# Keys, values and output weights split once and kept as halves in a scratch (one-core attention and expert layer)

## The chip, the cores and the metric

The kernel runs on one core of one Trainium2 chip; the chip's other cores do nothing. The metric is the device time of one execution in microseconds. The kernel before takes 2874.76 us (median of 3 runs, 2874.28 to 2878.58).

## The reference

x is (2, 2048, 2048), in all 4096 tokens of 2048 features, float32 throughout.

```python
xn = _layernorm(x, axis=-1)
# attention, one head, d = 512
qkv = einsum('bsc,cf->bsf', xn, Wqkv) + bqkv
attn = softmax(einsum('bqd,bkd->bqk', q, k) / sqrt(512))
out = einsum('bqd,dc->bqc', einsum('bqk,bkd->bqd', attn, v), Wo) + bo
# experts: 64 of rank 8, the best 16 gated by a softmax over q_r keys
z_gated = (xn @ A_w.T).reshape(..., 64, 8) * gate[..., None]
ffn = einsum('bsn,on->bso', z_gated, B_w) * (32 / 16)
x + out + ffn
```

## The kernel before

Every large product is taken in three passes, so that it comes out in nearly full precision: each float32 operand is split into a high part (rounded to fp32r by a ScalarE copy) and a low part (operand minus high part, a VectorE subtraction), and TensorE adds hi times hi, hi times lo and lo times hi into one PSUM bank (`three`, L1556 to L1558).

Phase A (`phase_a`, about the first 1377 us) normalizes x, multiplies by the joined weights and leaves k, q, v and z (the ungated, then gated expert activations) in DRAM scratches. The change does not touch it, except that its last items already start the first loads of phase B.

Phase B (`phase_b`) works through 8 turns t of 512 queries (`QG`); turns 0 to 3 belong to the first batch of 2048 tokens, turns 4 to 7 to the second. A turn has 32 items, in this order on TensorE:

- scores: 8 key items (K0 to K7 in this text), each 256 keys by 512 features;
- output of the turn before (u = t - 1): 16 items (O0 to O15), four for each block of 512 output columns: two with B_T for the expert part and two with Wo for the attention part. Turn 0 has none; the output of turn 7 comes at the very end;
- values: 8 value items (V0 to V7), each 256 keys by 512 features.

The softmax of turn t lies beside the output items of turn t - 1 (`softmax_step`): running maximum on VectorE, spread over the partitions by TensorE, subtraction of the maximum on VectorE (L1753), exponential on ScalarE (L1459), running sum on GpSimd (L1700). GpSimd also adds the output bias to the loaded x (L1691), and VectorE evicts the output banks with that sum (L1796).

Every item streams one operand through a ring of four slots (`RING`): SyncE loads 512 KB into `r_raw` (`fetch`, L1346), ScalarE makes `r_hi` (L1437), VectorE makes `r_lo` (L1725), TensorE multiplies and counts `b_used`. The fetch of item n waits until `r_lo` of item n - 4 is made; the ScalarE copy of item n waits until TensorE is done with item n - 4. Keys and values of a batch are thus loaded and split again in each of its four turns, and Wo and B_T in each of eight outputs: 256 items. All engines work through orders written out in the code; each engine's queue is served strictly in order. SyncE's queue also holds the loads of x into `res` (L1369), of z (L1406) and of the queries (L1350), and the stores of the result (L1361). `segments` runs turns 0 and 1 written out, turns 2 to 6 in a hardware loop, and turn 7 and the last output written out.

Of the kernel before, what the change touches and what calls it, by code (L numbers as in the profile page):

```python
# [20 lines left out]
F32 = mybir.dt.float32  # L21
# [3 lines left out]
P = 128  # L25
BANKS = 8
W = 512
# [3 lines left out]
def static(v):  # L31
    return isinstance(v, int)
# [28 lines left out]
def layer_kernel(nc, x, xT, W_blocks, b_cols, Wo, bo, B_T, WqT, keysT, out):  # L61
    T, C = x.shape
    D = Wo.shape[0]
    NE, RD = keysT.shape[1], keysT.shape[0]
    RANK = D // NE
    NB = 2
    S = T // NB
    KT = C // P
    TG = 1024
    NG = T // TG  # L70
    QG = 512
    NQ = T // QG
# [8 lines left out]
    stat_scr = nc.dram_tensor("stat_scratch", [NG, 2, TG], F32, kind="Internal").ap()  # L81
    t_scr = nc.dram_tensor("t_scratch", [4, 2, C // 2, W], F32, kind="Internal").ap()

    with ExitStack() as whole:
        def sb(name, shape, dt=F32):
            return whole.enter_context(nc.sbuf_tensor(name, shape, dt))

        psum = whole.enter_context(nc.psum_tensor("psum", [P, BANKS, W], F32))
        common = {
            "ident": sb("ident", [P, P]),  # L90
            "ones": sb("ones", [P, P]),
            "b_col": sb("b_col", [P, 3 * D // P]),
        }
        ahead = Programs()
# [3 lines left out]
        second = phase_b(nc, whole, psum, common, first, ahead, x, Wo, bo, B_T, k_scr, q_scr, z_scr, v_scr, out,  # L98
                         T, C, D, S, QG, NQ, KEYT, DT)
# [12 lines left out]
        @block.tensor  # L112
        def _(pe):
            first.tensor(pe)
            second.tensor(pe)

        @block.gpsimd
        def _(pool):
            first.gpsimd(pool)
            second.gpsimd(pool)  # L120

        @block.vector
        def _(dve):
            first.vector(dve)
            second.vector(dve)
# [1080 lines left out]
    return first  # L1206


def phase_b(nc, whole, psum, common, first, ahead, x, Wo, bo, B_T, k_scr, q_scr, z_scr, v_scr, out,
            T, C, D, S, QG, NQ, KEYT, DT):  # L1210
    RING = 4
    S_IT, O_IT, V_IT = KEYT // 2, 16, KEYT // 2
# [21 lines left out]
    def sem(name):  # L1234
        return whole.enter_context(nc.semaphore(name))
# [23 lines left out]

    b_const = sem("b_const")  # L1260
    b_raw = [sem(f"b_raw{i}") for i in range(RING)]
    b_hi = sem("b_hi")
    b_lo = sem("b_lo")
    b_used = sem("b_used")
# [42 lines left out]
    def uses(t, it):  # L1307

        n = number(t, it)
        if static(n):  # L1310
            return n // RING + 1
        return t * (PER // RING) + (it - O_IT) // RING + 1

    def segments(engine, scores, output, values):


        scores(0)
        values(0, True)
        scores(1)
        output(0, True)  # L1320
        values(1, True)
        with engine.Fori(2, NQ - 1) as t:
            scores(t)
            output(t - 1, True)
            values(t, True)
        scores(NQ - 1)
        output(NQ - 2, True)
        values(NQ - 1, False)
# [7 lines left out]
    def out_ready(engine, u, c, j):  # L1336
        if j < QT - 1:
            engine.wait_ge(b_o, u * CB * (QT - 1) + c * (QT - 1) + j + 1)
        else:
            engine.wait_ge(b_used, number(u + 1, S_IT + c * OPB + OPB - 1) + 1)  # L1340

    def sync(sp, early=False):
        def fetch(t, it, source):
            slot = it % RING
            wait(sp, b_lo, number(t, it) - RING + 1)
            sp.dma_start(r_raw[:, slot, :].rearrange("p (a w) -> p a w", a=source.shape[1]),  # L1346
                         source).then_inc(b_raw[slot], 16)

        def queries(t):
            sp.dma_start(q_raw[:], q_scr.rearrange("(m p) t -> p m t", p=P)[:, :, bass.ds(t * QG, QG)]  # L1350
# [46 lines left out]
        def values(t, more):  # L1397
            base = batch_base(t)
            for i in range(V_IT):
                fetch(t, S_IT + O_IT + i, v_scr[bass.ds(base + i * 2 * P, 2 * P), :]  # L1400
                      .rearrange("(a p) w -> p a w", p=P))
                if i == 0:
                    if static(t) and t == 0:
                        first.stored(sp)
                    wait(sp, b_zt, QT * t)
                    sp.dma_start(z_raw[:], z_scr[bass.ds(t * QG, QG), :]  # L1406
                                 .rearrange("(a p) w -> p a w", p=P)).then_inc(b_z, 16)
                    if more:
                        wait(sp, b_qlo, 2 * (t + 1))
                        queries(t + 1)  # L1410
                if not (static(t) and t == 0):
                    if i == 0:
                        store_block(t - 1, CB - 2)
                    if i == 4:
                        store_block(t - 1, CB - 1)

        if early:
            first.early_stored(sp)
# [135 lines left out]
    def tensor(pe):  # L1554
# [165 lines left out]

    def vector(dve, step=None):
        def split(t, it):
            slot = it % RING
            dve.wait_ge(b_hi, number(t, it) + 1)
# [191 lines left out]
```

## Time and profile before

| | |
|---|---|
| timed runs, median | 2874.76 us |
| profiled execution, its own time | 2878.93 us |
| its span, first to last instruction | 2877.1 us |
| mean granted clock of TensorE | 0.987 |
| TensorE (PE) busy | 2764.0 us, 96% |
| VectorE (DVE) busy | 1776.8 us, 62% |
| ScalarE (ACT) busy | 1053.9 us, 37% |
| GpSimd (POOL) busy | 425.0 us, 15% |
| HBM read, written | 390.74 MB, 83.91 MB |

The span is cut by the profile in 40 equal slices with the busy tenths of each engine; TensorE is at 9 tenths or more in nearly all of them from the sixth on, with a dip around 1440 us, which is turn 0 of phase B. The start-to-start distance of two matmuls in a full stretch is 0.227 us; their ends are modelled, and they overlap, so a single one reads 0.39 us.

### The profile page before, as it was taken

The numbers are of one execution on the slowest core, as the hardware profiler recorded it, in microseconds if no ns is written. First come the engines' busy times: TensorE is split into PE (matmuls) and PEld (weight loads), VectorE is DVE, ScalarE is ACT, GpSimd is POOL, SyncE is SP. The second block draws the span as 40 slices with busy tenths as digits, with TensorE's granted clock in tenths as the row PEclk, the third lists the DMA queues.
The fourth block names the chain that finished last, engine by engine and source line by source line (L and its number), as shares of the span: only waits on it lengthen the run. The fifth ranks groups of instructions, "written<-read, shape, count | busy, mean of one in ns | idle before, by whom it ended". The sixth has DMA issues, their size and how long they took to land.

```text
span 2877.1 us, 34126 instructions
## 1 busy us (share of the span) xinstructions
PE 2764.0 (96%) x12096; PEld 2249.8 (78%) x12096; DVE 1776.8 (62%) x2083; ACT 1053.9 (37%) x1354; POOL 425.0 (15%) x293
## 2 busy tenths in 40 slices
PE   6888999999999999999889999999999999999999
PEld 4676878878888888888778787887878878788787
DVE  6675876467646776455575666546566565565663
ACT  3552325522373223223343343333433334333331
POOL 0011000000000000000022405015041060320611
PEclk9899999999999999999999999999999999999999
DMA  7589765455555463324524534445344453444544
GB/s 296 180 314 301 231 199 191 146 164 174 190 198 142 143 201 121 103 95 154 176 88 139 183 107 163 148 149 186 102 155 151 138 191 116 142 162 128 183 132 139
DMA packets 263276, 476.35 MB, mean 166 GB/s; under 512 B 25328, under 2 KB 74608, under 8 KB 258928
## 3 DMA queue, kind: packets, MB, share of 16 engines
q1 hardware_dynamic: 229104, 387.13, 41.5%
q10 hardware_dynamic: 28288, 66.62, 6.7%
q0 software_dynamic: 5760, 20.97, 2.0%
q8 instruction: 74, 1.21, 0.2%
q14 instruction: 50, 0.41, 0.0%
HBM read 390.74 MB, written 83.91 MB: 165 GB/s over the span
## 4 chain that ended last, share of the span: by engine, by line
PE 81%; DVE 8%; DMA 4%; ACT 3%; issue 3%; POOL 1%; ACTq 0%; SPq 0%; DVEq 0%; POOLq 0%
PE psum L749 36%; PE psum L1556 14%; PE psum L1558 14%; PE psum L1557 14%; DVE prob L1753 2%; PE psum L686 2%; DVE r_lo L1725 2%; ACT r_hi L1437 1%; DMA stat_scratch<-mv 1%; DMA w_raw<-t_scratch 1%; DVE res L1796 1%; DMA rows<-x 1%; DVE w_lo L799 1%; PE psum L1676 0%; ACT w_hi L478 0%
## 5 line engine op out<-in xcount | busy, mean ns | idle before, releaser
L799 DVE TENSOR_TENSOR w_lo<-w_raw,w_hi 128x1024 fp32r<-128x1024 f32 x224 | 274.1, 1224 | 432.3 <-ACT w_hi L478 432.2
L478 ACT ACTIVATE w_hi<-w_raw 128x1024 fp32r<-128x1024 f32 x224 | 237.4, 1060 | 775.8 <-PE psum L749 681.9
L1725 DVE TENSOR_TENSOR r_lo<-r_raw,r_hi 128x1024 fp32r<-128x1024 f32 x256 | 384.1, 1514 | 189.7 <-ACT r_hi L1437 189.7
L1556 PE MATMUL psum<-r_hi,f_hi 128*128 128x512 f32 x1024 | 406.6, 397 | 27.6 <-DVE r_lo L1725 26.2
L1558 PE MATMUL psum<-r_hi,f_lo 128*128 128x512 f32 x1024 | 402.1, 393 | 0.0
L1557 PE MATMUL psum<-r_lo,f_hi 128*128 128x512 f32 x1024 | 402.1, 393 | 0.0
L749 PE MATMUL psum<-s_hi,w_hi 128*128 128x512 f32 x896 | 353.9, 395 | 27.5 <-DVE w_lo L799 15.8
L749 PE MATMUL psum<-w_hi,s_hi 128*128 128x512 f32 x896 | 351.9, 393 | 16.0 <-DVE w_lo L799 14.9
L749 PE MATMUL psum<-s_lo,w_hi 128*128 128x512 f32 x896 | 351.4, 392 | 0.0
L749 PE MATMUL psum<-w_lo,s_hi 128*128 128x512 f32 x896 | 351.2, 392 | 0.0
L749 PE MATMUL psum<-s_hi,w_lo 128*128 128x512 f32 x896 | 351.1, 392 | 0.0
L749 PE MATMUL psum<-w_hi,s_lo 128*128 128x512 f32 x896 | 351.0, 392 | 0.0
L1691 POOL TENSOR_TENSOR res<-res,b_out 128x512 f32<-128x512 f32 x128 | 219.9, 1748 | 664.2 <-DMA res<-x 664.2
L1437 ACT ACTIVATE r_hi<-r_raw 128x1024 fp32r<-128x1024 f32 x256 | 264.0, 1049 | 140.4 <-PE psum L1558 85.0
L1556 PEld LDWEIGHTS psum<-r_hi,f_hi 128*128 128x128 f32 x1024 | 194.1, 190 | 80.8 <-DVE r_lo L1725 24.3
L1558 PEld LDWEIGHTS psum<-r_hi,f_lo 128*128 128x128 f32 x1024 | 194.2, 190 | 41.4
L1557 PEld LDWEIGHTS psum<-r_lo,f_hi 128*128 128x128 f32 x1024 | 194.1, 190 | 39.3
L749 PEld LDWEIGHTS psum<-s_hi,w_hi 128*128 128x128 f32 x896 | 169.7, 189 | 68.9 <-issue 15.9
L1556 PE MATMUL psum<-p_hi,r_hi 128*128 128x512 f32 x512 | 208.1, 406 | 12.7 <-DVE p_lo L1845 8.0
L749 PEld LDWEIGHTS psum<-w_hi,s_hi 128*128 128x128 f32 x896 | 169.6, 189 | 56.6 <-DVE w_lo L799 16.9
L1700 POOL TENSOR_TENSOR run_sum<-prob 128x512 f32<-128x512 f32 x8 | 10.3, 1290 | 1367.8 <-ACT prob L1459 1367.8
L1558 PE MATMUL psum<-p_hi,r_lo 128*128 128x512 f32 x512 | 201.7, 394 | 0.0
(137 smaller groups left out, 4267.3 us busy)
## 6 DMA issues: line engine op xcount, KB each, us to landing
w_raw<-t_scratch SPq DMA_DIRECT2D x128, 512.0 KB, 4.0
w_raw<-W_blocks SPq DMA_DIRECT2D x96, 512.0 KB, 3.8
r_raw<-k_scratch SPq DMA_DIRECT2D x64, 512.0 KB, 3.8
r_raw<-v_scratch SPq DMA_DIRECT2D x64, 512.0 KB, 4.5
r_raw<-B_T SPq DMA_DIRECT2D x64, 512.0 KB, 3.9
res<-x SPq DMA_DIRECT2D x128, 256.0 KB, 4.8
r_raw<-Wo SPq DMA_DIRECT2D x64, 512.0 KB, 4.4
out<-res SPq DMA_DIRECT2D x128, 256.0 KB, 3.4
```

The lines of the kernel that those rows point to most:

```text
L478: nc.scalar.activation(w_hi[:, s % RAW], w_raw[:, s % RAW], ACT.Copy).then_inc(s_whi, 1)
L686: mm = pe.matmul(psum[0:M_R, bank, :], wq[:, block_k + k, :], t[:, k, :], start=(k == 0 and n == 0), stop=(k == HK - 1 and n == 1))
L749: mm = pe.matmul(psum[:, bank, :], stationary, moving, start=(k == 0 and n == 0 and not chained), stop=(k == HK - 1 and n == 2), skip_grou ...
L799: nc.vector.tensor_tensor(w_lo[:, s % RAW], w_raw[:, s % RAW], w_hi[:, s % RAW].bitcast(F32), ALU.subtract).then_inc(s_wlo, 1)
L1437: nc.scalar.activation(r_hi[:, slot, :], r_raw[:, slot, :], ACT.Copy).then_inc(b_hi, 1)
L1556: pe.matmul(bank, sh, mh, start=first, stop=False)
L1557: pe.matmul(bank, sh, ml, start=False, stop=False)
L1558: return pe.matmul(bank, sl, mh, start=False, stop=last)
L1691: nc.gpsimd.tensor_tensor(res[:, slot, :], res[:, slot, :], b_out[:, c * W:(c + 1) * W], ALU.add).then_inc(b_xb, 1)
L1725: nc.vector.tensor_tensor(r_lo[:, slot, :], r_raw[:, slot, :], r_hi[:, slot, :].bitcast(F32), ALU.subtract).then_inc(b_lo, 1)
L1753: nc.vector.tensor_tensor(prob[:, i, :], prob[:, i, :], max_all[:], ALU.subtract).then_inc(b_sub, 1)
L1796: nc.vector.tensor_tensor(res[:, tile % XO, :], psum[:, O_BANK[tile], :], res[:, tile % XO, :], ALU.add).then_inc(b_oev, 1)
```

## The change

A new DRAM scratch, `split_scr`, has a place for the two halves of 48 tiles. An item is split (`is_split`) as before where it is met first: the keys and values in turns 0 and 4, the output weights in turn 1. Behind the split, SyncE stores both halves (`keep`, two transfers of 512 KB). In all other turns SyncE loads the two halves from the scratch straight into `r_hi` and `r_lo`, once TensorE is done with the item four back and the stores out of that slot have landed; no ScalarE or VectorE instruction belongs to such an item, and TensorE waits for the landing itself. Items that are split wait on ScalarE for the stores of their slot too. `segments` has turn 4 written out between two hardware loops (turns 2 and 3, turns 5 and 6).

```diff
+    def is_split(t, it):
+        if not static(t) or t == NQ:
+            return False
+        if OUT_AT <= it < VAL_AT:
+            return t == 1
+        return t % BATCH == 0
...
+        turn(1)
+        LATE["loop"] = False
+        with engine.Fori(2, BATCH) as t:
+            turn(t)
+        turn(BATCH)
+        LATE["loop"] = True
+        with engine.Fori(BATCH + 1, NQ - 1) as t:
+            turn(t)
...
     def sync(sp, early=False):
+        def keep(t, it):
+            slot = it % RING
+            sp.wait_ge(b_lo, split_number(t, it) + 1)
+            for half, r in enumerate((r_hi, r_lo)):
+                sp.dma_start(split_scr[home(t, it), half], r[:, slot, :].bitcast(F32)).then_inc(b_keep[slot], 16)
...
         def fetch(t, it, source):
             slot = it % RING
-            wait(sp, b_lo, number(t, it) - RING + 1)
-            sp.dma_start(r_raw[:, slot, :].rearrange("p (a w) -> p a w", a=source.shape[1]),
-                         source).then_inc(b_raw[slot], 16)
+            if is_split(t, it):
+                earlier = in_slot(t, it)
+                if earlier and not is_split(*earlier[-1]):
+                    sp.wait_ge(b_used, number(t, it) - RING + 1)
+                wait(sp, b_lo, split_number(t, it) - RING + 1)
+                sp.dma_start(r_raw[:, slot, :].rearrange("p (a w) -> p a w", a=source.shape[1]),
+                             source).then_inc(b_raw[slot], 16)
+                keep_before(number(t, it) - RING + 1)
+                return
+            if static(t):
+                keep_before(number(t, it) - RING + 2)
+            sp.wait_ge(b_used, number(t, it) - RING + 1)
+            sp.wait_ge(b_keep[slot], 32 * kept(t, it))
+            for half, r in enumerate((r_hi, r_lo)):
+                sp.dma_start(r[:, slot, :].bitcast(F32), split_scr[home(t, it), half]).then_inc(b_raw[slot], 16)
...
     def scalar(act, step=None):
         def split(t, it):
+            if not is_split(t, it):
+                return
             slot, n = it % RING, number(t, it)
-            act.wait_ge(b_raw[slot], 16 * uses(t, it))
+            act.wait_ge(b_raw[slot], 16 * landed(t, it))
             wait(act, b_used, n - RING + 1)
+            wait(act, b_keep[slot], 32 * kept(t, it))
...
         def streamed(t, it):
-            pe.wait_ge(b_lo, number(t, it) + 1)
+            if is_split(t, it):
+                pe.wait_ge(b_lo, split_number(t, it) + 1)
+            else:
+                pe.wait_ge(b_raw[it % RING], 16 * landed(t, it))
```

VectorE in turn 7, from the spreading of the maximum on, beside O1 to O9. Before, L1725 is the split, L1753 the subtraction of the maximum, L1796 the eviction:

```order
L1744 TENSOR_REDUCE q_max<-psum 128x4
L1748 TENSOR_SCALAR diag<-ident,q_max 128x128 x4
L1725 TENSOR_TENSOR r_lo<-r_raw,r_hi 128x1024 x3
L1796 TENSOR_TENSOR res<-psum,res 128x512 x4
L1753 TENSOR_TENSOR prob<-prob,max_all 128x512 x2
L1725 TENSOR_TENSOR r_lo<-r_raw,r_hi 128x1024
```

The last two rows come four times before the next eviction. The changed kernel, where L1825 to L1834 and L1877 are the same instructions as L1744 to L1753 and L1796:

```order
L1825 TENSOR_REDUCE q_max<-psum 128x4
L1829 TENSOR_SCALAR diag<-ident,q_max 128x128 x4
L1877 TENSOR_TENSOR res<-psum,res 128x512 x4
L1834 TENSOR_TENSOR prob<-prob,max_all 128x512 x8
L1877 TENSOR_TENSOR res<-psum,res 128x512 x4
L1834 TENSOR_TENSOR prob<-prob,max_all 128x512 x8
```

All splits are gone from between them; the order of the rest is the same. SyncE at the start of phase B, turn 0, from the load of the bias to V1, before (L1346 is the fetch):

```order
L1380 DMA b_out<-bo 128x2048
L1346 DMA r_raw<-k_scratch 128x4x256 x4
L1346 DMA r_raw<-v_scratch 128x2x512
L1406 DMA z_raw<-z_scratch 128x4x512
L1350 DMA q_raw<-q_scratch 128x4x512
L1346 DMA r_raw<-v_scratch 128x2x512 x7
```

and in the changed kernel, the first rows (L1409 is the fetch of a raw tile, L1395 the store of a half):

```order
L1451 DMA b_out<-bo 128x2048
L1409 DMA r_raw<-k_scratch 128x4x256
L1395 DMA split_scratch<-r_hi 128x1024
L1395 DMA split_scratch<-r_lo 128x1024
L1409 DMA r_raw<-k_scratch 128x4x256
```

The four key fetches, which stood together, now have two stores behind each. SyncE in the changed kernel around V0 of turn 1 (L1418 loads a kept half, L1477 z, L1421 the queries, L1432 stores the result):

```order
L1409 DMA r_raw<-Wo 128x2x512
L1395 DMA split_scratch<-r_hi 128x1024
L1395 DMA split_scratch<-r_lo 128x1024
L1395 DMA split_scratch<-r_hi 128x1024
L1395 DMA split_scratch<-r_lo 128x1024
L1395 DMA split_scratch<-r_hi 128x1024
L1395 DMA split_scratch<-r_lo 128x1024
L1418 DMA r_hi<-split_scratch 128x1024
L1418 DMA r_lo<-split_scratch 128x1024
L1477 DMA z_raw<-z_scratch 128x4x512
L1421 DMA q_raw<-q_scratch 128x4x512
L1432 DMA out<-res 128x512 x4
```

The stores of O11, O12 and O13 stand ahead of the first kept load, and those of O14 and O15 follow ahead of the next two.

## Rows read from the trace of the kernel before

**Rows 1.** Windows: busy (count) of PE, PEld, DVE, ACT, POOL; clock; DMA; GB/s
```profile
1400.00:1492.00 92.00, 76.06 (x310) 60.82 (x309) 59.97 (x65) 38.67 (x58) 23.38 (x15) 0.89 0.27 88
1677.00:1862.00 185.00, 180.11 (x802) 147.19 (x801) 110.60 (x115) 66.62 (x91) 49.63 (x31) 1.00 0.45 149
```
**Rows 2.** Waits of PE, whole span, then 2100:2280: total, times, longest
```profile
PE psum L1556 <- DVE r_lo L1725: 26.2, 23, 1.9
...
PE psum L1556 <- DVE r_lo L1725: 3.4, 3, 1.8
```
**Rows 3.** Costliest groups, the page: busy, mean ns, idle before and releaser
```profile
L1725 DVE TENSOR_TENSOR r_lo<-r_raw,r_hi 128x1024 fp32r<-128x1024 f32 x256 | 384.1, 1514 | 189.7 <-ACT r_hi L1437 189.7
...
L1691 POOL TENSOR_TENSOR res<-res,b_out 128x512 f32<-128x512 f32 x128 | 219.9, 1748 | 664.2 <-DMA res<-x 664.2
L1437 ACT ACTIVATE r_hi<-r_raw 128x1024 fp32r<-128x1024 f32 x256 | 264.0, 1049 | 140.4 <-PE psum L1558 85.0
```
**Rows 4.** Timeline of PE in turn 3, O9: start, duration, instruction, idle before
```profile
1959.24 0.50 PE L1556 MATMUL psum<-r_hi,f_hi 128*128 128x512 f32 x1 [1.82 <-DVE r_lo L1725]
...
1961.25 0.63 PE L1557 MATMUL psum<-r_lo,f_hi 128*128 128x512 f32 x1
1961.68 0.63 PE L1558 MATMUL psum<-r_hi,f_lo 128*128 128x512 f32 x1
```
**Rows 5.** Windows: O7 to O13 of turns 2 and 7; turn 2: V0-V3, all O, all V
```profile
1760.68:1804.68 44.00, 39.25 (x169) 31.22 (x168) 34.95 (x29) 15.96 (x21) 35.43 (x22) 1.00 0.56 180
2683.93:2727.81 43.88, 40.58 (x170) 32.43 (x168) 34.88 (x29) 15.95 (x21) 35.13 (x22) 0.96 0.55 176
1815.56:1837.33 21.77, 21.77 (x98) 18.02 (x97) 10.97 (x14) 7.28 (x10) 0.00 (x0) 1.00 0.45 143
1720.73:1815.56 94.83, 89.94 (x397) 72.89 (x396) 56.83 (x55) 30.56 (x40) 43.69 (x27) 1.00 0.54 181
1815.56:1861.79 46.23, 46.23 (x212) 37.89 (x210) 28.16 (x31) 17.50 (x24) 0.00 (x0) 1.00 0.35 109
```
**Rows 6.** Timeline of DVE in turn 3, O6 to O8
```profile
1942.35 2.32 DVE L1725 TENSOR_TENSOR r_lo<-r_raw,r_hi 128x1024 fp32r<-128x1024 f32 x1 [1.65 <-ACT r_hi L1437]
1944.60 3.48 DVE L1753 TENSOR_TENSOR prob<-prob,max_all 128x512 f32<-128x512 f32 x2
...
1951.49 2.47 DVE L1796 TENSOR_TENSOR res<-psum,res 128x512 f32<-128x512 f32 x4
```
**Rows 7.** DMA queue and issues, the page: size, median us to landing
```profile
q1 hardware_dynamic: 229104, 387.13, 41.5%
...
r_raw<-k_scratch SPq DMA_DIRECT2D x64, 512.0 KB, 3.8
...
res<-x SPq DMA_DIRECT2D x128, 256.0 KB, 4.8
...
t_scratch<-xb SPq DMA_DIRECT2D x16, 512.0 KB, 8.4
```
**Rows 8.** SP's timeline at V0 of turn 3, and all loads of r_raw
```profile
1978.39 0.38 SPq L1346 DMA_DIRECT2D r_raw<-v_scratch  x1
...
DMA to landing us min/median/max: 3.4/4.0/11.0
```
**Rows 9.** Windows with the DMA engines full
```profile
1990.00:1995.00 5.00, 5.00 (x23) 4.14 (x23) 0.00 (x0) 0.89 (x1) 0.00 (x0) 1.00 1.05 395
...
250.00:260.00 10.00, 1.06 (x3) 0.77 (x3) 2.14 (x2) 3.23 (x4) 0.72 (x1) 0.70 1.06 249
```
**Rows 10.** Timelines of SP, ACT, DVE and PE, turn 0, K4
```profile
1388.32 2.26 SPq L1346 DMA_DIRECT2D r_raw<-k_scratch  x4
...
1394.64 1.06 ACT L1437 ACTIVATE r_hi<-r_raw 128x1024 fp32r<-128x1024 f32 x1 [5.70 <-DMA r_raw<-k_scratch]
1395.73 1.23 DVE L1725 TENSOR_TENSOR r_lo<-r_raw,r_hi 128x1024 fp32r<-128x1024 f32 x1 [6.06 <-ACT r_hi L1437]
...
1399.02 0.39 PE L1556 MATMUL psum<-q_hi,r_hi 128*128 128x512 f32 x1
```

More of the change, by code:

```diff
@@ L81, in layer_kernel @@
     stat_scr = nc.dram_tensor("stat_scratch", [NG, 2, TG], F32, kind="Internal").ap()
+    split_scr = nc.dram_tensor("split_scratch", [48, 2, P, 2 * W], F32, kind="Internal").ap()
     t_scr = nc.dram_tensor("t_scratch", [4, 2, C // 2, W], F32, kind="Internal").ap()
@@ L97, in layer_kernel @@
                             k_scr, q_scr, z_scr, v_scr, stat_scr, t_scr, ahead, T, C, D, NE, RD, RANK, KT, TG, NG)
-        second = phase_b(nc, whole, psum, common, first, ahead, x, Wo, bo, B_T, k_scr, q_scr, z_scr, v_scr, out,
+        second = phase_b(nc, whole, psum, common, first, ahead, x, Wo, bo, B_T, k_scr, q_scr, z_scr, v_scr, split_scr, out,
                          T, C, D, S, QG, NQ, KEYT, DT)
@@ L1206, in phase_a, with phase_b @@
     return first
-def phase_b(nc, whole, psum, common, first, ahead, x, Wo, bo, B_T, k_scr, q_scr, z_scr, v_scr, out,
+def phase_b(nc, whole, psum, common, first, ahead, x, Wo, bo, B_T, k_scr, q_scr, z_scr, v_scr, split_scr, out,
             T, C, D, S, QG, NQ, KEYT, DT):
@@ L1261, in phase_b @@
     b_raw = [sem(f"b_raw{i}") for i in range(RING)]
+    b_keep = [sem(f"b_keep{i}") for i in range(RING)]
     b_hi = sem("b_hi")
@@ L1305, in number, with turn_items, split_number, in_slot @@
         return PER * t - O_IT + it
[L1307 to L1312, printed above, removed]
-    def segments(engine, scores, output, values):
[L1317 to L1322, printed above, removed]
+    BATCH = S // QG
+    OUT_AT, VAL_AT = S_IT, S_IT + O_IT
+    assert NQ == 2 * BATCH and BATCH == 4
+    LATE = {"loop": False}
+    def is_split(t, it):
[4 more added lines that the diff above has]
+        return t % BATCH == 0
+    def turn_items(t):
+        return [(t, it) for it in range(PER) if not (t == 0 and OUT_AT <= it < VAL_AT)]
+    ITEMS = [item for t in range(NQ) for item in turn_items(t)]
+    ITEMS += [(NQ, it) for it in range(OUT_AT, VAL_AT)]
+    SPLITS = [item for item in ITEMS if is_split(*item)]
+    def split_number(t, it):
+        return SPLITS.index((t, it))
+    def in_slot(t, it):
+        return [item for item in ITEMS[:ITEMS.index((t, it))] if item[1] % RING == it % RING]
+    def landed(t, it):
+        if static(t):
+            return sum(1 if is_split(*item) else 2 for item in in_slot(t, it) + [(t, it)])
+        whole_turn = 2 * PER // RING
+        known = BATCH + 1 if LATE["loop"] else 2
+        return (t - known) * whole_turn + landed(known, it)
+    def kept(t, it):
+        known = t if static(t) else BATCH + 1 if LATE["loop"] else 2
+        return sum(is_split(*item) for item in in_slot(known, it))
+    def home(t, it):
+        if OUT_AT <= it < VAL_AT:
+            return 2 * 2 * S_IT + it - OUT_AT
+        batch = t // BATCH if static(t) else int(LATE["loop"])
+        return batch * 2 * S_IT + (it if it < S_IT else it - O_IT)
+    def segments(engine, scores, output, values):
+        def turn(t):
             scores(t)
@@ L1325, in segments @@
             values(t, True)
+        scores(0)
+        values(0, True)
+        turn(1)
[6 more added lines that the diff above has]
+            turn(t)
         scores(NQ - 1)
@@ L1340, in out_ready, with keep_before @@
             engine.wait_ge(b_used, number(u + 1, S_IT + c * OPB + OPB - 1) + 1)
+    KEPT = {"next": 0}
     def sync(sp, early=False):
+        def keep(t, it):
[3 more added lines that the diff above has]
+                sp.dma_start(split_scr[home(t, it), half], r[:, slot, :].bitcast(F32)).then_inc(b_keep[slot], 16)
+        def keep_before(n):
+            while KEPT["next"] < len(SPLITS) and number(*SPLITS[KEPT["next"]]) < n:
+                keep(*SPLITS[KEPT["next"]])
+                KEPT["next"] += 1
         def fetch(t, it, source):
             slot = it % RING
-            wait(sp, b_lo, number(t, it) - RING + 1)
-            sp.dma_start(r_raw[:, slot, :].rearrange("p (a w) -> p a w", a=source.shape[1]),
-                         source).then_inc(b_raw[slot], 16)
+            if is_split(t, it):
[7 more added lines that the diff above has]
+                return
+            if static(t):
+                keep_before(number(t, it) - RING + 2)
[3 more added lines that the diff above has]
+                sp.dma_start(r[:, slot, :].bitcast(F32), split_scr[home(t, it), half]).then_inc(b_raw[slot], 16)
         def queries(t):
@@ L1415, in values @@
                         store_block(t - 1, CB - 1)
+            if static(t) and t == BATCH:
+                keep_before(number(t + 1, 0))
         if early:
@@ L1722, in split @@
         def split(t, it):
+            if not is_split(t, it):
+                return
             slot = it % RING
-            dve.wait_ge(b_hi, number(t, it) + 1)
+            dve.wait_ge(b_hi, split_number(t, it) + 1)
             nc.vector.tensor_tensor(r_lo[:, slot, :], r_raw[:, slot, :], r_hi[:, slot, :].bitcast(F32),
```

## The prediction

> **What bounds the kernel now.** I read the busy shares first, then the list of PE's waits, then PE's own timeline around each wait. "Item" below is one use of the weight ring: 24 matmuls of 512 columns against one pair of tiles r_hi, r_lo. A turn is 512 queries: eight key items (K0 to K7), sixteen output items (O0 to O15) and eight value items (V0 to V7); turns 0 to 7, and sixteen output items behind the last.
>
> TensorE sets the pace: in an ordinary turn PE is busy 180.1 of 185 us, DVE 110.6, ACT 66.6 [rows 1]. So an engine that loses work gives time only where PE stands waiting for it. In the whole program PE waits 26.2 us, 23 times, for r_lo (L1725), and within one turn 3.4 us in 3 waits [rows 2]. That is the only wait of PE that comes back every turn, and r_lo is one of the two instructions that the change thins out [rows 3].
>
> The idle time is less than the loss. The timeline shows O9 starting after 1.82 us of idle; behind that the matmuls take 0.63 us instead of 0.39 (8 of them come 0.427 us apart, not 0.227) [rows 4]. That is TensorE at half its clock, 1.2 GHz for 2.4, after it had stood still for 1.82 us; the mean granted clock of such a stretch reads 0.96 [rows 5]. I therefore measure by windows. From the start of O7 to the start of O14 in turn 2 (seven items) it is 44.00 us; four undisturbed items, V0 to V3, take 21.77, so 5.44 each and 38.1 for seven [rows 5]. The loss is 5.9 us a turn. The same seven items of turn 7 take 43.88 us and lose 5.8.
>
> Why r_lo is late there: DVE is in a ring with ACT. It subtracts the maximum (L1753, two tiles a step), ACT takes the exponentials and only then r_hi, DVE idles 1.65 us for r_hi and then makes r_lo; and while POOL adds the bias, a split takes 2.3 us instead of 1.2 and a subtraction 1.7 [rows 6]. In the window of seven items DVE is busy 35 of 44 us and POOL 35 [rows 5]; with its idles of 1.65 us DVE is full. By the order of its instructions every r_lo leaves this stretch.
>
> **The change part by part.**
>
> Splits taken away. Of 256 pairs, 48 are still split: keys and values of turns 0 and 4, output weights of turn 1. 208 ACT copies (1.05 us each, 218 us) and 208 DVE subtractions (1.5 us, 312 us) go [rows 3]. Off PE's path nearly all of it is worth nothing. Where it counts is O8 to O12 in the turns whose output weights come ready made: turns 2 to 7. Six turns by 5.9 is 35.4 us. I count turn 4 in full, because its keys and values are split in stretches where PE never waited for r_lo.
>
> What would be late next in O8 to O12? PE then needs the landing (below) and the bank. Without splits DVE has, for four items (21.8 us), one block of four evictions (2.5 us) and eight subtractions (at most 1.74 each, 14 us) [rows 6]: 16.5 us, so evictions start when PE finishes the tile. ACT keeps eight exponentials and nothing else. I take no new wait.
>
> Turn 1: its output items are split as before, in the same loop of ACT and DVE, so its 5.9 us stay.
>
> The loads. A kept pair is two transfers of 512 KB, straight into the tiles PE reads, so it can't start before PE has finished the item four back: the lead is three items, 16.3 us, where before the raw tile went ahead of the split. A single 512 KB lands in 3.8 us [rows 7], so a lone pair takes about 3.8 + 1.05 MB at 395 GB/s = 6.5 us. Hidden. The worst place is V0, where SP issues a pair, z (1 MB), the queries (1 MB) and four stores (1 MB) at once: 4.2 MB. In the same place before, 5.8 MB were issued from 1978.4 on (five tiles of v, z, queries, stores) and the slowest load of r_raw took 11.0 us to land; the core moved 395 GB/s meanwhile [rows 8, 9]. With 4.2 MB queued, V1's pair, 5.44 us later, has 4.2 - 2.15 + 1.05 = 3.1 MB to wait for, 7.9 us, and about 2 more: 10 of 16.3. Hidden. Output items: 16 pairs (16.8 MB) and 8.4 MB of x and result in 88.9 us is 283 GB/s. Hidden at 395.
>
> The Trainium skill speaks against this: "DMA: Bandwidth & Descriptors", section "Where 436 GB/s comes from", puts transfers between HBM and SBUF at about 358 GB/s a core. The trace does not agree, for this one core running alone, with its 395 GB/s [rows 9]; by 358 the queue of turn 1's burst, below, would last 20.5 us instead of 18.6 and V1 there would be 4 us late, not 2.
>
> The stores of the halves (48 pairs, 96 transfers, 50 MB). Three places.
> Turn 0, keys: fetch of K4 is now followed by the store of K0, and ACT may split K4 only when that has landed. Before, SP issued K4 to K7 in one go at 1388.3; K4 landed 6.3 us later, r_hi began at 1394.64, r_lo ended at 1396.96 and PE wanted it at 1399.02 [rows 10]: 2.06 us of slack. The store puts 1.05 MB behind K4: 2.7 us at 395 GB/s. So 0.6 us late, and K5 to K7 are just in time. I take 1 us. Bounds: 0, and 4 if the stores go like t_scratch<-xb, which takes 8.4 us for 512 KB against 3.8 for a load [rows 7]. It falls ahead of the maxima, so it counts in full. Turn 0's values wait on softmax (PE is busy 76 of the 92 us from 1400 on [rows 1]) and their stores have two items of room: 0.
> Turn 1, output: per item 0.52 MB raw and 1.05 MB stored, with x and result 33.6 MB in the 94.8 us that such a stretch takes now [rows 5], 354 GB/s, under 395. But the stores of O13 to O15 stand among the burst of V0, so V1's pair ends a queue of 6.3 + 1.05 MB that started about 3 us late: 18.6 + 3 + 2 = 23.6 us after O13's start, wanted at 21.8. I take 2 us; bounds 0 and 6.
> Turn 4: its keys move 12.6 MB in 43.5 us (eight items), 289 GB/s; its values with z, queries and stores 16.8 MB in 46.2 [rows 5], 363 GB/s. Hidden.
>
> SP's order. SP now stays three items ahead of PE instead of up to seven. Behind its wait for b_used stand x loads, stores of the result, z and queries. x of a block is asked for six items before its eviction (33 us; landing 4.8 [rows 7], four additions of 1.7 on POOL [rows 3]): hidden. A wait for a landed store of the result may hold SP some 2 us, and the next fetch is due 5.4 later: 0. The loop becomes two loops with a written-out turn between; at the loop boundaries of the trace PE has no gap: 0.
>
> Sum against the profiled execution: 2878.93 - 35.4 + 1 + 2 = 2846.5. It lay 4.2 us over the median of the timed runs (2874.76), so 2842.3: **2842 us, 1.1% faster.**
>
> **Rivals.**
> A. Half given back to the stores. If the queues give 324 GB/s (q1: 387.13 MB in 41.5% of 2877 us [rows 7]) wherever stores are mixed in, turn 1's output takes 103.7 us instead of 94.8 (+9), and turn 4's values (16.8 MB) 51.8 instead of 46.2 (+6); with 1 in turn 0 and 2 in the burst the gain is 35.4 - 18 = 17: 2857. For: DMA is the only thing that grows. Against: 395 GB/s with stores in the mix.
> B. Slower: the weight ring becomes bound by DMA. One mechanism: reads and writes of the scratch at the 249 GB/s that the trace shows in 250:260 with all engines busy [rows 9]. Each output stretch then takes 25.2 MB / 249 = 101 us instead of 88.9: +12 in six turns, 9 behind the last; turn 1 135 instead of 94.8, +40; turn 4's keys +7, values +21. Together 149 - 35 = +114: 2989. It decides from about 290 GB/s down, where turn 1 and turn 4 alone cost 33 and the output stretches begin. Against: that stretch holds stores of 4 bytes an element and loads of one row spread over all partitions; here every descriptor row is 4 KB.
> C. No change, 2875: the wait for r_lo at O8 to O12 is only named so, and PE would stand there anyway for its bank (L1796 is in the same queue on DVE). For: DVE's slow stretch has POOL's 35 us in it, which stay. Against: in the trace evictions start right when PE ends a tile, and DVE loses its splits there, 2.3 us each.
> D. The change doesn't do what it says: ready pairs arrive later than PE asks because SP sits in a wait of its fixed order (b_st, b_oev). Each turn would lose 3 to 6 us, which is between A and C.
>
> **How the numbers follow.** Forecast 0.62 (2836 to 2851); A with D 0.18 (2851 to 2869); C 0.06; B 0.14, rather at its lighter end. What a measurement can tell from no change is 0.2%, 5.7 us: faster is below 2869, slower above 2880. Faster 0.80, same 0.06, slower 0.14. The range for eight in ten: from 2833 (all costs at their lower end, and turn 1 better by its own 5.9 us) to 2869. The forecast's own is 2836 to 2851.
>
> **What would show it.** PE's waits for r_lo: turns 2 to 7 none, turn 1 still about 4.7 us in four waits; a turn 178.7 us long instead of 184.7, no dip of the clock in it; O7 to O14 38.1 us. DVE's busy time down by about 300 us, ACT's by 218. Rates up to 390 GB/s in turn 1, about 283 in output stretches. PE waits for a landing only in V1, V2 of turn 1. It is wrong if PE shows landings of split_scratch as releaser in the plain turns, if items lengthen evenly beyond 5.44 us (B), or if O8 and O12 keep their gap with L1796 as releaser (C).

## The result, and the profile after

The changed kernel takes 2843.88 us (median of 4 runs, 2841.67 to 2844.22) against 2874.52 for the kernel before in the same comparison (2873.94 to 2878.58): ratio 0.9883, 95% interval 0.9868 to 0.9897. The forecast was 2842 us.

Windows are read as in [rows 1]: the stretch, its length, busy time (count) of PE, PEld, DVE, ACT and POOL, granted clock, DMA share, GB/s. Here are O7 to O13 of turn 2 and then the whole of turn 2, in the changed kernel; the first is to be held against [rows 5]:

```profile
1759.22:1797.30 38.08, 38.08 (x169) 31.53 (x168) 18.08 (x18) 7.08 (x12) 25.88 (x19) 1.00 0.83 282
1675.66:1854.41 178.75, 178.61 (x802) 147.30 (x800) 67.41 (x83) 36.12 (x59) 44.89 (x31) 1.00 0.70 247
```

The seven items take 38.08 us where they took 44.00, and PE has no idle in them, with DVE at 18 us instead of 35. The clock reads 1.00 in both: in turn 2 it had not fallen before either. The turn is 178.75 us; before, this stretch of the trace reads:

```profile
1677.08:1861.79 184.71, 179.82 (x802) 146.90 (x800) 110.60 (x115) 66.62 (x91) 49.63 (x31) 1.00 0.45 148
```

The waits of PE in the changed kernel from turn 2 to the end, which answer to [rows 2] (total, times, longest):

```profile
PE psum L1632 <- DMA r_lo<-split_scratch: 0.9, 1, 0.9
PE psum L1632 <- DVE attn L1855: 0.7, 1, 0.7
```

The wait for r_lo is gone from turns 2 to 7. In turns 0 and 1 it stays, with 1.7 us of it new, at K4 of turn 0:

```profile
PE psum L1632 <- DVE p_lo L1926: 6.7, 3, 2.4
PE psum L1632 <- DVE r_lo L1806: 5.0, 4, 1.9
```

Stretch by stretch, taken between the first matmuls of items in the two profiled executions:

| stretch | before | after | difference |
|---|---|---|---|
| until K0 of turn 0 | 1377.26 | 1376.53 | -0.7 |
| K0 to K3 of turn 0 | 21.76 | 23.59 | +1.8 |
| rest of turn 0 | 93.61 | 91.09 | -2.5 |
| turn 1 | 184.44 | 184.45 | 0.0 |
| turns 2, 3, 5, 6, 7 (each 184.4 to 184.7) | 923.13 | 893.56 | -29.6 |
| turn 4 | 184.68 | 179.73 | -4.9 |
| output of turn 7, to the end | 92.22 | 92.03 | -0.2 |
| span | 2877.1 | 2841.0 | -36.1 |

The rest of turn 0 scatters by itself, between 90.3 and 93.8 us in the later traces, whether halves are stored in it or not (best and best_again are one kernel, with 92.8 and 90.3); and phase A, which no kernel here changes but for the order of its last stores in one (best), ends between 1376.5 and 1388.0 us from one trace to another. So stretches of single traces are compared below inside the turns, where they repeat to 0.1 us.

### The profile page after: what moved, and what is told of

It reads as the page before. It is cut to its first block, busy times and chain, and to the rows that moved or that the text cites. A ratio compares the mean times of both kernels' runs of the same rounds, so it can differ in the third digit from the quotient of the medians.

```text
span 2841.0 us, 33300 instructions
## 1 busy us (share of the span) xinstructions
PE 2749.1 (97%) x12096; PEld 2244.6 (79%) x12096; DVE 1496.1 (53%) x1875; ACT 854.7 (30%) x1146; POOL 389.6 (14%) x293
## 4 chain that ended last, share of the span: by engine, by line
PE 85%; DVE 5%; DMA 4%; ACT 3%; issue 2%; SPq 0%; POOL 0%; ACTq 0%; DVEq 0%; POOLq 0%
PE psum L750 35%; PE psum L1632 15%; PE psum L1634 15%; PE psum L1633 15%; PE psum L687 2%; DMA stat_scratch<-mv 2%; DMA w_raw<-t_scratch 1%; ACT rows L534 1%; DVE prob L1834 1%; DMA w_raw<-W_blocks 1%; DVE r_lo L1806 1%; ACT w_hi L479 1%; DVE w_lo L800 1%; ACT rows L537 1%; PE psum L1755 0%
## 5 line engine op out<-in xcount | busy, mean ns | idle before, releaser
L1770 POOL TENSOR_TENSOR res<-res,b_out 128x512 f32<-128x512 f32 x128 | 183.5, 1463 | 798.3 <-DMA res<-x 798.2
L1877 DVE TENSOR_TENSOR res<-psum,res 128x512 f32<-128x512 f32 x128 | 86.9, 691 | 366.5 <-PE psum L1634 347.5
L1632 PE MATMUL psum<-q_hi,r_hi 128*128 128x512 f32 x512 | 200.0, 391 | 2.5 <-DVE r_lo L1806 1.7
L1633 PE MATMUL psum<-p_lo,r_hi 128*128 128x512 f32 x512 | 201.2, 393 | 0.0
```

The lines of the kernel that those rows point to most:

```text
L1632: pe.matmul(bank, sh, mh, start=first, stop=False)
L1633: pe.matmul(bank, sh, ml, start=False, stop=False)
L1770: nc.gpsimd.tensor_tensor(res[:, slot, :], res[:, slot, :], b_out[:, c * W:(c + 1) * W], ALU.add).then_inc(b_xb, 1)
L1877: nc.vector.tensor_tensor(res[:, tile % XO, :], psum[:, O_BANK[tile], :], res[:, tile % XO, :], ALU.add).then_inc(b_oev, 1)
```

## Experiments

Eleven kernels ran in three comparisons, one of them in two (best, best_again). The kernel before took 2879.8 to 2880.8 us in these, 5 to 6 us more than in the first, so their times are given with the ratio to it (95% interval). Five (b_nobias, extra1, extra2, lead2, lead1) ran once, without a ratio; their traces carry what is said.

### Which of the kept tiles bring the time

**out_only** keeps the output weights alone, **kv_only** the keys and values alone. Both have all turns written out, since a count of splits in a hardware loop would need other waits.

```diff
-        if not static(t) or t == NQ:
-            return False
-        if OUT_AT <= it < VAL_AT:
-            return t == 1
-        return t % BATCH == 0
+        weights = OUT_AT <= it < VAL_AT
+        return not weights or t == 1
+
+    def is_stored(t, it):
+        weights = OUT_AT <= it < VAL_AT
+        return is_split(t, it) and (weights)
```

`is_stored` takes the place of `is_split` where SyncE stores halves and counts the stores. In kv_only the two results are `weights or t % BATCH == 0` and `is_split(t, it) and (not weights)`.

> All eight turns written out, no loop. Only the output weights are kept as halves (split in turn 1, loaded as halves in turns 2 to 7 and in the last output); keys and values are split again in every turn, as before. Theory 1, the time came from the r_lo waits at O8 to O12 alone, so keys and values contribute nothing: the whole gain, 2840 to 2844 us, no late K4 in turn 0 and no late K0 in turn 5. Rival, relief of DVE and ACT as a whole: about a third of the gain, since a third of the kept traffic stays (88 of 208 kept items are gone): 2855 to 2865.

> All eight turns written out. Only keys and values are kept as halves; the output weights are split in every output, as before. Theory 1: no gain, 2874 to 2879 us (2 us of late K4 in turn 0, perhaps DMA waits), with r_lo waits of about 3.4 us in every turn and 44 us for O7 to O13. Rival, general relief: 2850 to 2862.

out_only: 2848.03 us, 0.9891 (0.9872 to 0.9909). kv_only: 2882.11 us, 1.0005 (0.9995 to 1.0014). Turn 2 of each, O7 to O13 and then the turn; first out_only:

```profile
1769.38:1807.45 38.07, 38.07 (x169) 31.54 (x168) 16.25 (x17) 6.56 (x11) 24.75 (x18) 1.00 0.82 285
1685.95:1864.56 178.61, 178.60 (x802) 147.32 (x800) 86.46 (x99) 51.37 (x75) 43.15 (x31) 1.00 0.59 200
```

kv_only, with its one line of PE's waits in that turn:

```profile
1766.78:1810.66 43.88, 39.31 (x170) 31.22 (x168) 33.75 (x28) 15.95 (x22) 35.13 (x22) 1.00 0.42 137
1683.30:1867.76 184.46, 179.88 (x801) 146.99 (x800) 92.39 (x99) 51.39 (x75) 50.44 (x31) 1.00 0.56 194
```

```profile
PE psum L1626 <- DVE r_lo L1800: 4.6, 4, 1.9
```

Keeping keys and values takes 18 us of DVE's work out of a turn (110.6 to 92.4) and brings nothing; keeping the output weights takes 24 us out and brings 6 us a turn. The median of out_only lies above its forecast of 2840 to 2844, on a trace whose phase A ended 11 us later than that of the changed kernel (1388.0); its turns are what was expected. Relief of DVE as a whole is out as a reason; the place of the split decides. (The rival's time in the expectation of out_only rests on a slip: 112 of the 208 kept items stay there and 96 are gone, so over half of the gain and not a third would have been its mark. The whole gain was measured, so the reading is the same.)

### The late keys of turn 5

**all_written** has the changed kernel's turns all written out.

```diff
-        with engine.Fori(2, BATCH) as t:
-            turn(t)
-        turn(BATCH)
-        LATE["loop"] = True
-        with engine.Fori(BATCH + 1, NQ - 1) as t:
-            turn(t)
+        for t in range(1, NQ - 1):
+            turn(t)
...
-            if static(t) and t == BATCH:
-                keep_before(number(t + 1, 0))
```

> The changed kernel with all turns written out instead of two loops of two turns, so that SyncE need not wait for the last split of turn 4 before it loads the first kept keys of turn 5. If that wait is what made K0 of turn 5 late (0.9 us idle, 1.16 in all): 1 us less than the changed kernel, 2842 to 2843, and turn 5 begins without a gap. If the longer program costs instruction fetches, gaps of PE named issue and a longer time.

2845.29 us, 0.9887 (0.9869 to 0.9905); from the changed kernel that can't be told apart by time. By the trace it can: turn 4 takes 178.62 us, not 179.73, and its values have no wait behind them. In the changed kernel SyncE's timeline (start, duration, instruction) around the end of turn 4 was:

```profile
2198.59 0.43 SPq L1395 DMA_DIRECT2D split_scratch<-r_lo  x1
...
2204.16 0.32 SPq L1395 DMA_DIRECT2D split_scratch<-r_hi  x1
2204.52 0.43 SPq L1395 DMA_DIRECT2D split_scratch<-r_lo  x1
2205.22 0.56 SPq L1418 DMA_DIRECT2D r_hi<-split_scratch  x1
2205.82 1.17 SPq L1418 DMA_DIRECT2D r_lo<-split_scratch  x1
```

and PE's:

```profile
2212.87 0.49 PE L1632 MATMUL psum<-q_hi,r_hi 128*128 128x512 f32 x1 [0.88 <-DMA r_lo<-split_scratch]
```

SyncE waited for the halves of V7, ready at 2204.1, and issued their stores before it asked for the first pair of keys, so that this pair's lead was 7 us and not 16.3. The program being longer cost nothing: no gap named issue beside the one of 4.7 us that every kernel here has in turn 0. The turns of the loops read 178.74 there and 178.6 written out: 0.14 us each.

### Why r_lo was late: the chain of ACT and DVE

**b_swap** keeps nothing; it is the kernel before with another order on ScalarE.

```diff
             for i in range(O_IT):
-                split(u + 1, S_IT + i)
+                if i < EXP_STEP or not softmax:
+                    split(u + 1, S_IT + i)
                 if softmax:
+                    if EXP_STEP <= i + 1 < O_IT and i >= EXP_STEP:
+                        split(u + 1, S_IT + i + 1)
                     softmax_step(u + 1, i)
+                    if i == EXP_STEP - 1:
+                        split(u + 1, S_IT + EXP_STEP)
```

> The kernel before, nothing kept. One thing changed: in the output stretch from O4 on ScalarE copies r_hi of the next item ahead of the two exponentials of this step, not behind them, so VectorE need not idle 1.65 us per item for the chain subtraction, exponentials, copy. If the waits came from that chain of ACT and DVE: DVE gains about 8 x 1.65 us in the stretch, more than PE's 3.4 us of waits, and the time falls to 2835 to 2845 with no scratch at all. If DVE's own work beside POOL (35 of 44 us) is the bound: less than a third of the gain, 2865 to 2874.

2839.21 us, 0.9868 (0.9848 to 0.9887): with nothing kept, no scratch, no store and no load more, the whole gain, and turn 1's besides. Turn 2, O7 to O13 and the turn:

```profile
1756.34:1794.42 38.08, 38.08 (x169) 31.54 (x168) 36.11 (x27) 14.05 (x19) 36.15 (x21) 1.00 0.62 205
1672.79:1851.53 178.74, 178.60 (x802) 147.32 (x800) 118.66 (x115) 66.89 (x91) 54.90 (x31) 1.00 0.47 153
```

DVE is busier than ever, 36 of 38 us, and PE never waits. DVE's timeline in that stretch (start, duration, instruction) shows why; compare [rows 6]:

```profile
1765.28 3.48 DVE L1758 TENSOR_TENSOR prob<-prob,max_all 128x512 f32<-128x512 f32 x2
1768.68 2.32 DVE L1730 TENSOR_TENSOR r_lo<-r_raw,r_hi 128x1024 fp32r<-128x1024 f32 x1
1770.92 3.48 DVE L1758 TENSOR_TENSOR prob<-prob,max_all 128x512 f32<-128x512 f32 x2
1774.33 2.32 DVE L1730 TENSOR_TENSOR r_lo<-r_raw,r_hi 128x1024 fp32r<-128x1024 f32 x1
```

A step takes 5.64 us without the idle of 1.65, where in [rows 6] it takes 7.37, from 1942.35 to the next split:

```profile
1949.72 1.84 DVE L1725 TENSOR_TENSOR r_lo<-r_raw,r_hi 128x1024 fp32r<-128x1024 f32 x1 [1.65 <-ACT r_hi L1437]
```

PE needs a pair each 5.44 us. So a step is still 0.2 us over PE's pace, and that and the evictions between the steps eat only a lead that was there: PE has no wait for r_lo in the whole trace.

**b_nobias** takes the other part of the cause away: the kernel before without GpSimd's additions, so it leaves the output bias out of the result.

```diff
-                nc.gpsimd.tensor_tensor(res[:, slot, :], res[:, slot, :], b_out[:, c * W:(c + 1) * W],
-                                        ALU.add).then_inc(b_xb, 1)
+                pool.sem_inc(b_xb, 1)
```

> The kernel before without GpSimd's addition of the output bias (128 additions of 1.7 us; the bias bo is left out of the result). Theory, the waits at O8 to O12 need both: the chain of ACT and DVE and DVE instructions stretched from 1.2 to 2.3 us and from 0.68 to 1.77 beside GpSimd. Then DVE's stretched ones go but for the running sums, and turns take 178.7 instead of 184.7 us, time 2835 to 2842. If the chain alone makes them: turns stay at 184 or at most fall by 2 us.

One run, 2846.49 us; turns of 180.1 us. The chain is still there and idles as long, but the subtractions are short again:

```profile
1765.53 2.31 DVE L1724 TENSOR_TENSOR r_lo<-r_raw,r_hi 128x1024 fp32r<-128x1024 f32 x1 [1.65 <-ACT r_hi L1437]
1767.76 1.28 DVE L1752 TENSOR_TENSOR prob<-prob,max_all 128x512 f32<-128x512 f32 x2
1770.69 2.32 DVE L1724 TENSOR_TENSOR r_lo<-r_raw,r_hi 128x1024 fp32r<-128x1024 f32 x1 [1.65 <-ACT r_hi L1437]
```

5.16 us a step, under PE's 5.44. The 1.3 us per turn that are left come with the evictions: one wait of 1.0 us at O9 in each turn, behind the step that has four evictions in it and takes 7.57 us. So 4.6 of the 5.9 us a turn hang on the bias additions, and all 5.9 on the idle of 1.65 us. With the additions gone a step falls from 7.37 us to 5.16, under PE's pace, and with the idle gone to 5.64, which the lead of the ring covers; with both in it the lead is used up and PE waits. One thing I had not expected is that r_lo stays at 2.3 us with the bias gone, beside GpSimd's running sums. The Trainium skill, "SBUF — State Buffer", section "Who interferes with whom", says that a DVE instruction with two SBUF inputs contends with a GpSimd instruction that reads SBUF, and one with at most one SBUF input, outside the two-port perf modes, does not. The trace agrees on both: r_lo takes 1.22 us alone and 2.3 beside GpSimd, the subtraction 0.68 and 1.77, while the evictions, whose second input is in PSUM, stay between 0.67 and 0.69 us.

### What the loads can bear

**extra1** and **extra2** are all_written with one or two more loads of 512 KB for each output item, into the idle r_raw, in turns 2, 3, 5, 6 and 7. The function below is called behind the fetch of every output item; an extra load waits on SyncE until the last one into its slot has landed.

```diff
+        def extra(t, it):
+            for slot in (it % RING, (it + 2) % RING)[:EXTRA]:
+                wait(sp, b_extra[slot], 16 * EX[slot])
+                sp.dma_start(r_raw[:, slot, :], split_scr[home(t, it), 0]).then_inc(b_extra[slot], 16)
+                EX[slot] += 1
```

> The changed kernel written out, with one more load of 512 KB per output item into the unused r_raw in turns 2, 3, 5, 6 and 7: the output stretches then ask for 25.2 + 8.4 = 33.6 MB in 88.8 us, 378 GB/s, or 3.1 MB per two items. If the trace's 395 GB/s is what the queues give: still hidden, turns at 178.6 us or up to 2 us longer from bursts. If the queues give 358 GB/s or less: 94 us and more per stretch, each of the five turns at least 5 us longer, 2870 and over.

> As the one before with two more loads per output item: 42 MB in a stretch of 88.8 us, 473 GB/s, more than any row of the trace. The stretch is then bound by DMA, and its length gives the rate: 42 MB / 395 = 106 us, so each of the five turns 17 us longer, 196 us, time 2925 to 2935. At 358 GB/s: 117 us, turns 207 us, 2985. If loads run ahead and take from the value and key stretches, less.

extra1 ran once, 2850.83 us; its turns take 178.6 us, like those of all_written, so the difference in time lies ahead of turn 1 (phase A ended 2.3 us later than in the trace of all_written, and turn 0 took 2.9 us more). extra2: 2888.43 us; the five turns with the loads take 182 to 188 us, turn 4 178.6. The output stretch of turn 2, extra1:

```profile
1729.15:1817.88 88.73, 88.72 (x397) 73.32 (x396) 35.82 (x39) 13.24 (x22) 41.91 (x30) 1.00 0.98 362
```

extra2, the output stretch and the values behind it:

```profile
1730.35:1820.83 90.48, 89.03 (x397) 73.22 (x396) 33.09 (x39) 13.25 (x22) 42.89 (x31) 1.00 1.03 407
1820.83:1872.97 52.14, 48.08 (x211) 38.99 (x210) 17.69 (x22) 10.82 (x17) 0.00 (x0) 0.97 0.71 262
```

At 362 GB/s over 89 us the weight ring doesn't notice. At 407 the queues are full, and PE waits 25.9 us in eleven waits for r_lo of the scratch, 18.0 us of it not in the stretch but behind it, at V1, where the backlog meets the burst at V0. The 17 us a turn of the expectation were too much: of what didn't fit (42 MB asked, 36.8 moved) most was moved in the value stretch, which had room (262 GB/s over 52.14 us, 13.7 MB; the changed kernel moves 223 over 46.23 there, 10.3 MB). The changed kernel's own stretches, turn 1 (with the stores) and turn 2:

```profile
1534.83:1629.45 94.62, 91.31 (x397) 74.20 (x396) 56.03 (x55) 27.71 (x37) 44.69 (x28) 0.98 0.94 341
1719.32:1808.18 88.86, 88.72 (x397) 73.28 (x396) 34.28 (x39) 13.26 (x22) 42.10 (x30) 1.00 0.79 277
```

**lead2** and **lead1** load a kept pair one and two items later than the changed kernel.

```diff
-            sp.wait_ge(b_used, number(t, it) - RING + 1)
+            sp.wait_ge(b_used, number(t, it) - RING + 1 + 1)
             sp.wait_ge(b_keep[slot], 32 * kept(t, it))
```

In lead1 it is `+ 1 + 2`.

> The changed kernel, but a kept pair is loaded only when TensorE is done with the item three back, so the lead is two items (10.9 us) and not three (16.3). In the output stretches a pair lands in about 5 us: hidden. In the burst at V0 (4.2 MB queued) the pair of V1 should take about 10 us by the sum of the prediction: 0 to 3 us of waiting per turn at V1 and V2, turns 178.7 to 182, time 2844 to 2862. If landing really takes the 14.7 us that was the slowest in the changed kernel: 4 us and more per turn, 2870.

> As the one before with a lead of one item (5.44 us). A lone pair needs about 4.9 to 6.5 us to land, so every kept item should wait 0.5 to 2 us, 208 items: 100 to 400 us more, and 10 us more in each burst at V0: 3000 to 3300. It tells how far the changed kernel is from being bound by its loads; if landing were hidden even then, 2850.

lead2: 2860.36 us, one run; turns 2, 3, 5 and 6 take 180.1 to 180.7 us, turn 1 191.0, turn 7 178.6. Turns 2, 3, 5 and 6 have one wait each at V1, of 1.1 to 1.6 us; turn 7 has none, and the late keys of turn 5 stay (0.85 us). Here turn 1's and turn 2's:

```profile
1644.21 0.50 PE L1632 MATMUL psum<-p_hi,r_hi 128*128 128x512 f32 x1 [4.72 <-DMA r_lo<-split_scratch]
...
1826.42 0.50 PE L1632 MATMUL psum<-p_hi,r_hi 128*128 128x512 f32 x1 [1.62 <-DMA r_lo<-split_scratch]
```

With a lead of 10.9 us a wait of 1.6 means that V1's pair takes 12.5 us in a plain turn, where the prediction's sum said 10. In turn 1 it was asked for at 1629.34 and landed at 1644.2, 14.8 us later, and SyncE had come to it 0.9 us late. lead1: 2978.74 us, turns 1 to 7 of 194 to 199 us, 89.0 us in 65 waits for the scratch. So 5.4 us of lead is too little by 16 to 20 us a turn from turn 2 on, not for each item: a lone pair often lands within it. The third item of lead is what hides the burst.

### The three faults together

**best** is all_written with b_swap's order on ScalarE and one edit at SyncE: K4 of turn 0 is fetched, and K0's halves are stored, before phase A's last sixteen stores and the load of the bias.

```diff
+                if not (static(t) and t == 0 and i < RING):
+                    fetch_keys(t, i, base)
                 if static(t) and t == 0 and i == RING:
                     first.last_store(sp)
                     sp.dma_start(b_out[:], bo.rearrange("(a d) -> a d", a=1).to_broadcast([P, C])
                                  ).then_inc(b_const, 16)
-                if not (static(t) and t == 0 and i < RING):
-                    fetch_keys(t, i, base)
```

> The changed kernel with three edits: all turns written out; SyncE fetches K4 of turn 0 and stores the halves of K0 before it takes up the last stores of phase A and the load of the bias, not behind them; and ScalarE copies r_hi of the next item ahead of the exponentials from O4 on (matters in turn 1 alone). If K4 was late only for the queue ahead of K0's stores: K0 to K3 of turn 0 take 21.8 us again, not 23.4 to 23.6. Turn 1 takes 178.6 instead of 184.4. In all 9 us less than the changed kernel, 2835 to 2838; against the ScalarE reorder alone (2839.2) 1 to 3 us less, since the loop boundaries cost 0.1 us each and nothing else is left to win. If the stores cost turn 1 or turn 0 elsewhere, no better than 2839.

2839.53 us, 0.9854 (0.9837 to 0.9870). K0 to K3 of turn 0, best and all_written:

```profile
1382.15:1403.91 21.76, 21.76 (x98) 18.03 (x97) 10.49 (x20) 4.54 (x7) 0.00 (x0) 1.00 0.92 304
```

```profile
1381.40:1404.78 23.38, 21.93 (x98) 17.84 (x96) 9.17 (x19) 4.42 (x7) 0.00 (x0) 1.00 0.93 317
```

All three faults (r_lo late in turn 1, K4 late in turn 0, K0 late in turn 5) are mended in the trace, turns 1 to 7 take 178.6 us each, and the time is no more than level with b_swap's. **b_swap_written** (b_swap with the turns written out, as in all_written) and the same kernel **best_again** were compared once more on one chip.

> The kernel before with the ScalarE reorder and all turns written out, nothing kept. If written-out turns save the 0.1 us per turn seen in the changed kernel and nothing more: 2838 to 2840, turns of 178.6. It has the whole gain of the best kernel with keeping in it, so the same time within 1.5 us.

> The kernel with keeping, both queue edits and the ScalarE reorder once more, on the same chip as the version without keeping: the two within 0.1% of each other. If keeping is worth something by itself behind the reorder, this one is faster by over 3 us; if its stores cost, slower by as much.

b_swap_written: 2840.98 us, 0.9858 (0.9841 to 0.9874). best_again: 2840.94 us, 0.9866 (0.9850 to 0.9883). Their turns agree to 0.05 us. Once ScalarE's order is right, keeping the halves is worth nothing that can be measured, and costs nothing either. All of them beat the kernel before by 1.3 to 1.5%. Their medians (2839.2 to 2841.0) lie below those of the changed kernel and of all_written (2843.9 and 2845.3), whose intervals of the ratio overlap with theirs; what tells them apart is turn 1, 178.6 us for 184.4.

## Why the prediction was right, point by point

- **What bounds the kernel, and the 5.9 us a turn.** Right, in place and in size. O7 to O13 take 38.08 us in turns 2 to 7; out_only and kv_only show that these turns pay for the output weights alone. Measuring by windows and not by the list of waits (3.4 us a turn) was what made the size right.
- **The half clock as the rest of the loss.** Wrong, though the size doesn't hang on it. The 44.00 us were taken in turn 2, and there the clock never fell: behind the same gap of 1.82 us the matmuls keep their distance of 0.227 us.

```profile
1774.53 0.50 PE L1556 MATMUL psum<-r_hi,f_hi 128*128 128x512 f32 x1 [1.82 <-DVE r_lo L1725]
1774.86 0.40 PE L1557 MATMUL psum<-r_lo,f_hi 128*128 128x512 f32 x1
...
1776.70 0.39 PE L1556 MATMUL psum<-r_hi,f_hi 128*128 128x512 f32 x1
1776.92 0.39 PE L1557 MATMUL psum<-r_lo,f_hi 128*128 128x512 f32 x1
```

Turn 2 has four waits for r_lo in place of three, 4.75 us in all (44.00 less 39.25 busy in [rows 5]); turn 3 has three of 3.37 us and the half clock between them:

```profile
1945.40:1989.38 43.98, 40.61 (x169) 32.44 (x168) 34.92 (x29) 15.95 (x21) 35.39 (x22) 0.96 0.55 182
```

Both windows take 44.0 us and both turns 184.7. What sets their length is the chain of ACT and DVE; a slower PE only waits less for it. The rest of the loss is behind each gap: a first matmul stands 0.34 us before the next and not 0.227, and idle is counted from a modelled end 0.39 us after the last start, not 0.227. That is 0.28 us for each of four gaps, 1.1 us, and 4.75 + 1.1 is the 5.9. kv_only bears it out: clock up and four waits of 4.6 us in turns 1 to 6, clock down and three waits of 3.3 us in turn 7, all of them 184.4 to 184.5 us long.

- **Six turns, not seven, and turn 4 in full.** Right: turn 1 stays at 184.45 us. Turn 4 won 6.1 in its output stretch and lost 1.1 behind it.
- **Why r_lo is late.** Right in its parts, shown by b_swap and b_nobias. I had read from them only that the splits must leave the stretch. The same rows said that 7.37 us a step, less the 1.65 of idle, is 5.72, near enough to PE's 5.44; the cheaper cure was in sight.
- **No new wait at O8 to O12.** Right; rival C is out.
- **Loads hidden.** Right, with less room than the sum said: 12.5 us for V1's pair in turn 2 of the changed kernel (asked for at 1797.50, landed at 1809.98), not 10. The sum took DMA at its full rate of 395 GB/s from the first byte, 2.15 MB in the 5.44 us before that pair; the trace has 223 GB/s in 1792.0:1797.5, 1.2 MB, and the 0.9 MB between them are 2.3 us. Stores of the result landed in 7.2 us (median) in the changed kernel, where they took 3.4.
- **Turn 0, 1 us.** Mechanism right, size small: 1.8 us. The stores of K0 did land 2.5 us behind K4, near the 2.7 reckoned (1395.1 and 1397.6), but K4 itself landed 7.5 us after its issue, not 6.3: 2.5 and 1.2, less the slack of 2.06, come to the gap of 1.67 us. The clock stayed up behind it.
- **Turn 1, 2 us at V1.** Wrong by those 2 us: V1's r_lo landed 14.7 us after its issue at 1620.01, at 1634.7, and PE came to it at 1634.9. It was as near as that, 0.2 us; lead2 shows what lies behind it. The sum had V1's pair landing 23.6 us after O13's start, and it was 21.6. The term that failed is the start of the queue: put 3 us behind O13's start, it was 0.3 us behind it (1613.34).
- **Turn 4 hidden.** Wrong by 1.1 us: the step "at the loop boundaries of the trace PE has no gap: 0" looked at PE alone and not at the line that makes SyncE store V7's halves before it goes round. The difference in SyncE's order would have shown it.
- **Sum.** The steps came to -32.4 us on the profiled execution, the trace says -36.1: -35.6 in turns 2 to 7 without the late pair, +1.8 and +1.1 for the two late pairs, and -3.4 in phase A, the rest of turn 0 and the last output, which is scatter. Without the scatter it is -32.7. That the sum came so near is part luck: 2 us too many in turn 1 stand against 0.8 too few in turn 0 and 1.1 in turn 4. The runs differ by 30.6 us, medians of 4; the profiled execution of the kernel before lay 4.4 us over its median, that of the changed kernel at its own.
- **The signs.** DVE's busy time fell by 281 us (about 300 said), ACT's by 199 (218 said). The splits took 313 us less on DVE, as reckoned, but the subtraction of the maximum rose from 131.8 to 148.4 us: 63 of its 128 instructions now take the 1.77 us that they take beside GpSimd, where 45 did before. Rates: 402 GB/s in 1540:1550 of turn 1 (390 said), 277 in the output stretch of turn 2 (283 said). PE's one wait for a landing was at K0 of turn 5, not at V1 or V2 of turn 1.
- **Rivals.** A: no, 341 GB/s with stores in turn 1's output stretch and no wait for a landing there. B: no; extra2 shows its mechanism at work, but the bound lies somewhere over the 362 GB/s of extra1, where PE had no such wait, and not at 290. (Rows of x and of the result are 2 KB, not 4, so that argument against B was only half true.) D: no, though SyncE's order did make the one wait of turn 5.

What stays open: the scatter of phase A between traces (1376.5 to 1388.0 us) was not looked into, turn 1's values were not run without their stores, and nothing here tells why the clock falls behind O9's gap in one turn and not in another.

## What to carry to other kernels

Where one engine waits for another in a step, write the step's time on that engine out, idle included, and set it against the pace of the engine that bounds: if the busy part alone would keep up, or nearly, turn the order inside the chain before taking work away. When work is taken away by storing its result, only the copies that stand in the late stretch pay (16 of 48 tiles here); and the lead of a direct load has to be judged at its worst burst, not on its median landing.

## What the runs showed of the hardware

- The DMA queues of this one core gave 407 GB/s over the 90 us of an output stretch when they were kept full (extra2), above the 395 of [rows 9], with loads and stores mixed in rows of 2 and 4 KB.
- The length of a gap alone did not tell whether TensorE's clock would fall. Behind the gap of 1.82 us at O9 of turn 3 it fell to half [rows 4]; behind the gap of 1.82 us at O9 of turn 2 in the same trace it stayed up, and in kv_only it stayed up behind gaps of 1.93 to 1.94 us in turns 1 to 6 and fell behind one of 1.94 us in turn 7. It also stayed up behind 0.88 us at K0 of turn 5 and 1.67 us at K4 of turn 0 in the changed kernel.
- Some issues held SyncE long: a store of r_hi (median of 48: 0.47 us) 3.26 us at 1391.98. In the changed kernel's trace the five longest, 2.3 to 3.3 us, all came with seven to nine transfers issued and not yet landed; most issues with as many under way were short (median 0.5 us), so the long queue is a condition at most, and the cause stays open.
- Beside GpSimd's two-input instructions a VectorE subtraction of 1024 columns took 2.3 us for 1.22 and one of 512 columns 1.77 for 0.68, while evictions with one input in PSUM stayed at 0.67 to 0.69 us.
